# A graph layer with experts on one core: GpSimd writes a small buffer and waits for that write behind each gather and scatter

## The chip, the cores and the metric

The kernel runs on one core of a Trainium2 chip. The time is the device time of one execution in microseconds (us). Engines are named as in the profile: PE is the matmul engine, PEld its weight loads, DVE the vector engine, ACT the scalar engine, POOL is GpSimd, SP the engine that here only issues transfers. Each engine works through its own instructions in order; they wait for each other through semaphores.

## What is computed

There are 6250 nodes with 256 features and 100000 edges, sorted by target node. First a graph layer, then a mixture of experts, both with a residual:

```python
h = layernorm(x)
msg_sum = segment_sum(h[src], dst, N)
deg = segment_sum(ones, dst, N)
agg = msg_sum / maximum(deg, 1)
x = x + concatenate([h, agg], 1) @ W.T + b
xn = layernorm(layernorm(x)) * gamma + beta
logits = xn @ Wr + br                  # 8 experts, the 2 best are taken
w = softmax(top_2(logits))
x = x + sum over the 2 of  w_e * (gelu(xn @ W1[e] + b1[e]) @ W2[e] + b2[e])
```

## The kernel before

**The head** loads x in seven parts, normalises it and writes it to DRAM as `h_rows`, and works out from the edge list which edge tile adds to which node tile.

**The stream** is a loop over a time step t (`for t in range(END)`), which every engine runs through in its own function with its own instructions. Up to STEPS = 830, each t is one step of the segment sum: 128 edges, whose rows of `h_rows` GpSimd has gathered into SBUF with one indirect DMA of 128 rows of 1 KB (L662); PE multiplies them by a one-hot matrix (L764, two passes for float32, so 1660 matmuls) into one of three PSUM banks; DVE adds the bank to the node tile in `acc` (L1125). The first 48 gathers serve two steps each, so there are 782 gathers for 830 steps. The first 63 gathers go to places of their own (`region`); after that they go round a ring of 17 places (`work`). Gather g into the ring's place waits until the step that read the place before is summed (`summed.wait(pool, t - RING)`), and PE waits for the landing of each gather (`got`).

When a node tile is complete, the layer's product, the layernorm, the logits and the choice of experts follow for it a few steps later, on PE, ACT and DVE, between the steps of the sum. Node tiles are closed in 12 batches. For each batch GpSimd scatters its rows to the experts' queues in DRAM, two indirect DMAs for each node tile (L673), one at each t from SCATTER[b] on, so that a scatter comes behind a gather; there are 98. Tiles of 128 queue rows are fetched by SP, multiplied by the expert's weights (L833, L858) and written back as answers, also between the steps of the sum.

**The tail** starts at t = STEPS: the last batches, the remaining experts' tiles, and for each node tile two gathers of its answers (L685, 98), the weighted sum on DVE, and the store of the output.

GpSimd thus has in its stream, in order: 782 gathers with 88 of the scatters among them, then 10 scatters, then 98 gathers of answers. It does nothing else there. The order is written out by hand; no scheduler changes it. `Own(nc, name, engine)` (L31) is a semaphore that an engine raises and waits for itself: `then(i)` lets instruction i raise it and makes the engine wait until it has.

Of the kernel before, what the change touches and what calls it, by code (L numbers as in the profile page):

```python
# [12 lines left out]
P = 128  # L13
# [35 lines left out]
def build(nc, x, src, dst, gnn_w, gnn_b, gamma, beta, wr, br, w1, b1, w2, b2, out):  # L49
    pe, dve, act, pool, sp = nc.tensor, nc.vector, nc.scalar, nc.gpsimd, nc.sync  # L50
# [13 lines left out]
    STEPS = ET + NT - 1  # L64
# [29 lines left out]
    CLEAR = 3  # L94
    FETCH = 6
    PACE = 7


    SIZES = [6, 6, 6, 5, 5, 5, 4, 2, 5, 3, 1, 1]
# [30 lines left out]
    def sb(name, shape, dt=F32):  # L130
        return nc.alloc_sbuf_tensor(name, shape, dt)
# [76 lines left out]
    pslot_i = sb("pslot_i", [1, X], I32)  # L208
    zcol = sb("zcol", [P, 1])
    padrow = sb("padrow", [P, ROW])  # L210
    pcol_i, step_i, qbase_i, e_idx = sb("pcol_i", [P, 1], I32), sb("step_i", [P, GB], I32), sb("qbase_i", [P, X], I32), sb("e_idx", [P, GB], I32)
    bound = sb("bound", [P, 2])

# [109 lines left out]
    d_own, a_own, g_own = Own(nc, "d_own", dve), Own(nc, "a_own", act), Own(nc, "g_own", pool)  # L323
# [20 lines left out]
    def gathered(t):  # L344

        return t - SHARED if t >= BOTH else t // 2 if t % 2 == 0 else None

    def place_of(g):

        return early[:, g, :] if g < SHARED + EXTRA else grow[:, (g - SHARED - EXTRA) % RING, :]  # L350
# [14 lines left out]
    def size(b):  # L365
        return BATCHES[b][1] - BATCHES[b][0]
# [12 lines left out]
    for b in range(NB):  # L379
        t = SCATTER[b] + 2 * size(b) + 7 if SCATTER[b] < STEPS else max(PLACES[b] + 8, STEPS + 5)  # L380
        for j in range(UPTO[b], UPTO[b + 1]):
            if begin_at:
                t = max(t, begin_at[-1] + (PACE if begin_at[-1] + PACE < STEPS else 3))
            begin_at.append(STEPS if STEPS - CLEAR <= t < STEPS else t)
# [12 lines left out]
    def backs(t):  # L397

        return [r for r in range(NT) if BACK[r] == t]

    def back(r, s):

        return grow[:, place_in_ring(STEPS - RING + 2 * (r % PAIRS) + s), 0:D]
# [4 lines left out]
    def answered(engine, j):  # L408

        if j >= 0:  # L410
            engine.wait_ge(s_answer, 16 * (j + 1))
# [226 lines left out]
    def gpsimd_head():  # L638
# [9 lines left out]
        for g in range(GB):  # L648
            pool.indirect_dma_start(tab_i[0:GS, g, :], None, comb, bass.IndirectOffsetOnAxis(e_idx[0:GS, g:g + 1], 0)).then_inc(s_tab, 16)

    def gpsimd_stream():
        pool.wait_ge(s_hst, 16 * NLB)
        srcs_up.wait(pool)
        for t in range(END):
            g = gathered(t) if t < STEPS else None
            if g is not None:
                if g >= RING:
                    pool.wait_ge(got[g % RING], 16 * (g // RING))
                if g >= SHARED + EXTRA + RING:
                    summed.wait(pool, t - RING)  # L660
                cell_of = CELLS + g if g < SHARED else t
                pool.indirect_dma_start(place_of(g)[:, 0:D], None, h_rows,  # L662
                                        bass.IndirectOffsetOnAxis(srcs[:, cell_of:cell_of + 1], 0)).then_inc(got[g % RING], 16)
            for b in range(NB):
                for n in range(2 * size(b)):
                    if t == SCATTER[b] + n:
                        if n == 0:
                            place_up.wait(pool, b)
                            if b == FLUSH + 1:
                                pool.wait_ge(s_pad, 16 * (X + 1))  # L670
                            if b == NB - 1:
                                pool.wait_ge(s_pad, 16 * (2 * X + 1))
                        pool.indirect_dma_start(queue, bass.IndirectOffsetOnAxis(place_i[:, b % 2, n % 2, n // 2:n // 2 + 1], 0),  # L673
                                                pay[:, b % 2, n // 2, :], None).then_inc(s_sent[b], 16)
            for r in backs(t):
                if r == 0:
                    answered(pool, FIRST_TILES - 1)
                if r == CUT:
                    answered(pool, ALL_TILES - 1)
                if r < PAIRS:  # L680
                    summed.wait(pool, STEPS - RING + 2 * r + 1)
                whole_up.wait(pool, r - PAIRS)
                answer_up.wait(pool, r)
                for s in range(2):
                    pool.indirect_dma_start(back(r, s), None, answers[r >= CUT],  # L685
                                            bass.IndirectOffsetOnAxis(answer_i[:, s, r:r + 1], 0)).then_inc(s_pair[r % PAIRS], 16)
# [507 lines left out]
    sync_stream()  # L1194
    scalar_stream()
    gpsimd_stream()
    tensor_stream()
    vector_stream()
# [24 lines left out]
```

## Time and profile before

| | us |
|---|---|
| median of 3 runs | 1425.81 |
| the 3 runs | 1423.88, 1425.81, 1431.27 |
| span of the profiled execution, first to last instruction | 1787.5 |
| PE busy in it | 1241.8 |
| POOL busy in it | 948.0 |
| DVE busy in it | 812.6 |
| ACT busy in it | 463.2 |

The profiled execution is 361.7 us, or 25%, longer than the median of the runs. Its rows give durations and waits of that execution; of the runs only the whole time is known. A row of a timeline gives start, duration, engine, line, operation and tiles; in brackets behind it stands how long the engine was idle before it and what ended that. "issue" there is idle time for which the profile shows no wait, and "remote" one that was ended by something that the profile can't name.

### The profile page before, as it was taken

How to read it: one execution, taken by the hardware profiler on the slowest of the kernel's cores; microseconds unless marked ns; L12 is line 12 of the kernel's file. 1: busy time of each engine (PE TensorE's matmuls, PEld its weight loads, DVE VectorE, ACT ScalarE, POOL GpSimd, SP SyncE). 2: the span in 40 equal slices, each digit the busy share in tenths (PEclk: the TensorE clock that was granted, in tenths of full speed). 3: DMA queues.
4: the chain of work that ended last, by engine and by line, in shares of the span. 5: the costliest groups of instructions: out<-in, count | busy, mean ns of one | idle time of the engine just before them, and what ended most of it. 6: DMA issues, size and time to landing. Idle time of an engine off the chain costs nothing.

```text
span 1787.5 us, 23229 instructions
## 1 busy us (share of the span) xinstructions
PE 1241.8 (69%) x5751; PEld 942.1 (53%) x5751; DVE 812.6 (45%) x2587; ACT 463.2 (26%) x1019; POOL 948.0 (53%) x995
## 2 busy tenths in 40 slices
PE   3223777765874778678787688688788868795881
PEld 2101343442652556556566566566666656684771
DVE  8312663452444445344434444445366565642333
ACT  4200000210220134124124224233322413463440
POOL 3574035666556655655655655665556565115544
PEclk9855998777886889898888889888889889997886
DMA  9732044433333333343333333343344333324553
GB/s 335 247 104 64 1 153 151 133 99 100 110 99 94 107 111 106 115 121 95 113 111 101 110 112 104 109 122 101 115 128 120 105 109 107 101 78 132 160 159 119
DMA packets 128488, 212.63 MB, mean 119 GB/s; under 512 B 25378, under 2 KB 94295, under 8 KB 128119
## 3 DMA queue, kind: packets, MB, share of 16 engines
q0 software_dynamic: 48352, 129.18, 25.2%
q1 hardware_dynamic: 77561, 81.17, 13.7%
q8 instruction: 52, 0.85, 0.2%
q10 hardware_dynamic: 2446, 0.80, 0.2%
q14 instruction: 77, 0.63, 0.1%
HBM read 167.37 MB, written 50.87 MB: 122 GB/s over the span
## 4 chain that ended last, share of the span: by engine, by line
PE 44%; another core or an unknown queue 17%; issue 16%; DVE 11%; ACT 6%; DVEq 2%; DMA 2%; POOL 1%; ACTq 0%; POOLq 0%
PE psum L764 16%; PE psum L833 9%; PE psum L858 8%; DVE acc L1125 5%; PE psum L777 4%; ACT expert_buf L633 2%; PE psum L812 2%; PE psum L778 1%; ACT expert_buf L625 1%; PE psum L845 1%; ACT region L570 1%; DVEq L1118 1%; PE psum L806 1%; PE psum L789 1%
## 5 line engine op out<-in xcount | busy, mean ns | idle before, releaser
L662 POOL DMA_INDIRECT work<-h_rows,srcs x719 | 681.0, 947 | 576.3 <-PE psum L764 324.0
L1125 DVE TENSOR_TENSOR acc<-acc,psum 128x257 f32 x830 | 350.3, 422 | 713.5 <-PE psum L764 329.1
L764 PE MATMUL psum<-work 128*128 128x257 f32 x1438 | 483.6, 450 | 193.7 <-DVE acc L1125 121.9
L764 PEld LDWEIGHTS psum<-work 128*128 128x128 f32 x1438 | 274.7, 219 | 300.3 <-issue 279.1
L833 PE MATMUL psum<-expert_buf 128*128 128x128 f32 x1792 | 235.3, 288 | 40.5 <-ACT expert_buf L625 34.3
L833 PEld LDWEIGHTS psum<-expert_buf 128*128 128x128 f32 x1792 | 230.3, 203 | 50.4 <-ACT expert_buf L625 36.7
L858 PE MATMUL psum<-region,expert_buf 128*128 x896 | 244.7, 422 | 11.6 <-issue 6.5
L633 ACT ACTIVATE expert_buf<-psum,b_col 128x128 f32<-128x128 f32 x448 | 127.8, 370 | 429.7 <-remote 220.0
L858 PEld LDWEIGHTS psum<-region,expert_buf 128*128 128x128 f32 x896 | 186.2, 216 | 49.9 <-issue 21.6
L764 PE MATMUL psum<-region,work 128*128 (+1 forms) x222 | 81.2, 486 | 106.0 <-issue 67.0
L999 DVE TENSOR_TENSOR work<-psum,rel 128x1152 f32<-128x1152 f32 x98 | 126.3, 1289 | 53.6 <-issue 36.7
L685 POOL DMA_INDIRECT work<-answers,answer_i x98 | 93.0, 949 | 108.2 <-DMA answers<-expert_buf 43.5
L625 ACT COPY expert_buf<-region 128x1024 f32 x112 | 117.6, 1050 | 108.7 <-remote 48.2
L673 POOL DMA_INDIRECT queue<-pay,place_i x98 | 97.4, 994 | 85.9 <-DVE place_i L1040 57.7
L580 ACT ACTIVATE acc<-acc,rdeg 128x256 f32<-128x256 f32 x49 | 25.1, 513 | 363.1 <-DVE rdeg L1131 229.5
L777 PE MATMUL psum<-wgt,pair_t 128*128 128x256 f32 x392 | 106.2, 419 | 17.2 <-ACT pair_t L584 11.4
L764 PEld LDWEIGHTS psum<-region,work 128*128 128x128 f32 x222 | 40.8, 220 | 146.0 <-issue 144.0
L1183 DVE TENSOR_TENSOR expert_buf<-psum,b_bc 128x256 f32<-128x256 f32 x112 | 47.2, 422 | 128.2 <-PE psum L858 59.2
L777 PEld LDWEIGHTS psum<-wgt,pair_t 128*128 128x128 f32 x392 | 82.8, 214 | 36.1 <-ACT pair_t L584 15.1
L662 POOL DMA_INDIRECT region<-h_rows,srcs x63 | 59.6, 946 | 35.0 <-issue 18.9
L627 ACT COPY expert_buf<-psum 128x256 f32<-128x256 f32 x112 | 41.6, 371 | 84.8 <-PE psum L845 48.6
L812 PEld LDWEIGHTS psum<-wr_sb,xn_t 128*128 128x128 f32 x196 | 34.6, 242 | 34.8 <-ACT xn_t L610 19.0
(248 smaller groups left out, 896.3 us busy)
## 6 DMA issues: line engine op xcount, KB each, us to landing
expert_buf<-queue SPq DMA_DIRECT2D x112, 128.0 KB
answers<-expert_buf SPq DMA_DIRECT2D x112, 128.0 KB
work<-h_rows,srcs POOLq DMA_INDIRECT x719
region<-in_L_ffn_W_dram SPq DMA_DIRECT2D x16, 512.0 KB
h_rows<-region SPq DMA_DIRECT2D x7, 896.0 KB
own<-h_rows SPq DMA_DIRECT2D x49, 128.0 KB
own<-x_rows SPq DMA_DIRECT2D x49, 128.0 KB
out_dram<-acc SPq DMA_DIRECT2D x49, 128.0 KB
```

What stands on the lines that cost most here:

```text
L625: w1c_up.up(act.copy(w1_now, w1_sb[:, ds(e, 1), :, :].rearrange("p a c h -> p (a c) h")))
L633: i = act.activation(gel[j % 2][:, k * P:(k + 1) * P], hidden(j)[:, k * P:(k + 1) * P], ACT.Gelu, bias=b1_col[:, ds(e + k * X, 1)])
L662: pool.indirect_dma_start(place_of(g)[:, 0:D], None, h_rows, bass.IndirectOffsetOnAxis(srcs[:, cell_of:cell_of + 1], 0)).then_inc(got[g % ...
L673: pool.indirect_dma_start(queue, bass.IndirectOffsetOnAxis(place_i[:, b % 2, n % 2, n // 2:n // 2 + 1], 0), pay[:, b % 2, n // 2, :], None ...
L685: pool.indirect_dma_start(back(r, s), None, answers[r >= CUT], bass.IndirectOffsetOnAxis(answer_i[:, s, r:r + 1], 0)).then_inc(s_pair[r % ...
L764: summed.up(pe.matmul(STEP_BANKS[t % BANKS][:, 0:GW], hot[:, k, :], rows, start=True, stop=True))
L777: pe.matmul(PAIR[:, 0:D], pair_t[:, c * P:(c + 1) * P], wgt[:, c, :], start=(c == 0), stop=False)
L812: i = pe.matmul(ROUTE[:, D + n * X:D + (n + 1) * X], xn_t[:, c * P:(c + 1) * P], wr_sb[:, c, :], start=(c == 0), stop=(c == DC - 1))
L833: i = pe.matmul(hidden(j)[:, units], w1_now[:, c, units], xt[j % 2][:, c * P:(c + 1) * P], start=(c == 0), stop=(c == DC - 1))
L858: i = pe.matmul(result(j), gel[j % 2][:, k * P:(k + 1) * P], w2_sb[:, ds(e, 1), k, :].rearrange("p a o -> p (a o)"), start=(k == 0), stop= ...
L999: hot_up.up(dve.tensor_tensor(hot[:, k0:k0 + n, :], COUNT[:, 0:P].unsqueeze(1).broadcast_to([P, n, P]), rel[:, first:first + n].unsqueeze( ...
L1125: added.up(dve.tensor_tensor(sums, sums, STEP_BANKS[t % BANKS][:, 0:GW], ALU.add))
```

## The change

A scratch buffer of 128 partitions by 24 float32 columns is added. Behind each gather of the stream, and behind each scatter at a step before STEPS, GpSimd writes zeros to it and waits until that write is complete, before it goes on to its next instruction. Nobody reads the buffer. The 10 scatters and 98 gathers of the tail have no such write.

```diff
+    PAUSE = 24
...
+    pause = sb("pause", [P, PAUSE])
...
+    def rest():
+        g_own.then(pool.memset(pause[:, :], 0.0))
+
     def gpsimd_stream():
...
                 pool.indirect_dma_start(place_of(g)[:, 0:D], None, h_rows,
                                         bass.IndirectOffsetOnAxis(srcs[:, cell_of:cell_of + 1], 0)).then_inc(got[g % RING], 16)
+                rest()
...
                         pool.indirect_dma_start(queue, bass.IndirectOffsetOnAxis(place_i[:, b % 2, n % 2, n // 2:n // 2 + 1], 0),
                                                 pay[:, b % 2, n // 2, :], None).then_inc(s_sent[b], 16)
+                        if t < STEPS:
+                            rest()
```

On GpSimd, in the first batch of scatters, the kernel before has gathers (DMA work) and scatters (DMA queue) in turn, directly behind each other; in brackets stands what each waits for:

```order
L662 DMA work<-h_rows,srcs 128x256 [waits summed,got8]
L673 DMA queue<-pay,place_i 54656x256
L662 DMA work<-h_rows,srcs 128x256 [waits summed,got9]
L673 DMA queue<-pay,place_i 54656x256
L662 DMA work<-h_rows,srcs 128x256 [waits summed,got10]
```

In the changed kernel, on GpSimd at the start of a batch of scatters (the lines are 5 or 6 higher):

```order
L667 DMA work<-h_rows,srcs 128x256 [waits summed,got1,g_own]
L654 MEMSET pause 128x24
L679 DMA queue<-pay,place_i 54656x256 [waits place_up,g_own]
L654 MEMSET pause 128x24
L667 DMA work<-h_rows,srcs 128x256 [waits summed,got2,g_own]
L654 MEMSET pause 128x24
L679 DMA queue<-pay,place_i 54656x256 [waits g_own]
```

Between any two of them a write has come in, and the wait for it (`g_own`) is one more wait of the DMA that follows. There are 870 such writes: 782 behind gathers and 88 behind scatters. No instruction of another engine is added or moved.

## Rows read from the trace of the kernel before

**Rows 1.** Busy us of each engine in four stretches; (x) counts instructions.
```profile
core 0: us, PE busy (x) PEld busy (x) DVE busy (x) ACT busy (x) POOL busy (x), PEclk, DMA share, GB/s
59.00:139.00 80.00, 19.75 (x40) 9.71 (x40) 11.03 (x21) 0.00 (x0) 60.09 (x64) 0.62 0.44 134
139.00:243.00 104.00, 63.33 (x193) 32.56 (x193) 52.39 (x113) 0.51 (x1) 15.55 (x18) 0.81 0.15 48
243.00:1515.00 1272.00, 955.38 (x4296) 719.89 (x4297) 598.38 (x1862) 325.33 (x704) 752.61 (x790) 0.85 0.38 112
1515.00:1787.00 272.00, 185.36 (x1129) 166.22 (x1127) 101.96 (x367) 104.10 (x256) 102.74 (x108) 0.85 0.41 124
```
**Rows 2.** Timeline of POOL where the ring is first full, and just behind it.
```profile
157.22 0.94 POOL L662 DMA_INDIRECT work<-h_rows,srcs  x1 [0.30 <-issue]
158.47 0.94 POOL L662 DMA_INDIRECT work<-h_rows,srcs  x1 [0.30 <-issue]
242.99 0.94 POOL L662 DMA_INDIRECT work<-h_rows,srcs  x1 [83.57 <-PE psum L764]
244.23 0.94 POOL L662 DMA_INDIRECT work<-h_rows,srcs  x1 [0.30 <-PE psum L764]
245.48 0.94 POOL L662 DMA_INDIRECT work<-h_rows,srcs  x1 [0.30 <-PE psum L764]
```
**Rows 3.** Timeline of POOL, a gather behind a scatter and a scatter behind that.
```profile
388.52 1.00 POOL L673 DMA_INDIRECT queue<-pay,place_i  x1 [0.30 <-issue]
389.82 0.97 POOL L662 DMA_INDIRECT work<-h_rows,srcs  x1 [0.30 <-PE psum L764]
391.09 1.00 POOL L673 DMA_INDIRECT queue<-pay,place_i  x1 [0.30 <-issue]
```
**Rows 4.** Waits of POOL from 243 to 1515: us in total, times, longest.
```profile
POOL work L662 <- PE psum L764: 324.0, 189, 83.6
POOL work L662 <- issue: 172.6, 477, 4.1
POOL work L662 <- remote: 74.5, 36, 3.1
```
**Rows 5.** Timeline of POOL at the start: its only short writes.
```profile
0.29 0.10 POOL L1211 MEMSET const-float32-1.0<- 128x1 f32 x1
0.32 0.11 POOL L1211 MEMSET const-bfloat16-1.0<- 128x1 bf16 x1
...
0.86 0.86 POOL L639 IOTA work<- 128x888 int32 x1 [0.40 <-POOLq L1211]
1.68 0.12 POOL L640 IOTA pcol_i<- 128x1 int32 x1
1.76 0.12 POOL L641 IOTA step_i<- 128x8 int32 x1
...
1.92 4.59 POOL L643 MEMSET acc<- 128x5397 f32 x1
```
**Rows 6.** Timeline: DVE's write that releases a scatter, and DVE's waits for itself.
```profile
544.47 0.17 DVE L1040 TENSOR_TENSOR place_i<-place,trash 128x12 int32<-128x12 f32 x1
...
544.91 0.99 POOL L673 DMA_INDIRECT queue<-pay,place_i  x1 [0.56 <-DVE place_i L1040]
...
545.86 0.17 DVE L1053 CAST cnt_i<-cnt 128x8 int32<-128x8 f32 x1
546.07 0.17 DVE L1054 TENSOR_SCALAR cnt_i<-cnt_i 128x8 int32<-128x8 int32 x1
```
**Rows 7.** Timeline of a stretch in which PE and DVE stand while POOL issues.
```profile
569.32 0.96 POOL L662 DMA_INDIRECT work<-h_rows,srcs  x1 [0.30 <-issue]
570.43 0.42 DVE L1125 TENSOR_TENSOR acc<-acc,psum 128x257 f32 x1 [4.78 <-remote]
570.59 1.00 POOL L673 DMA_INDIRECT queue<-pay,place_i  x1 [0.30 <-remote]
...
571.00 1.20 PE L764 MATMUL psum<-work 128*128 128x257 f32 x2 [3.54 <-issue]
...
573.16 1.00 POOL L673 DMA_INDIRECT queue<-pay,place_i  x1 [0.30 <-issue]
...
575.21 1.20 PE L764 MATMUL psum<-work 128*128 128x257 f32 x2 [3.02 <-issue]
```
**Rows 8.** Groups of instructions from 243 to 1515: busy, mean ns, idle before and releasers.
```profile
L1125 DVE TENSOR_TENSOR acc<-acc,psum 128x257 f32 x702 | 296.3, 422 | 590.2 <-PE psum L764 310.6 <-remote 183.6 <-issue 54.9
```

## The prediction, made before the changed kernel was run

> **What bounds the kernel now.** I read the busy time of each stretch first [rows 1], then the timeline of POOL [rows 2, 3] and its waits [rows 4]. The change touches GpSimd alone, so the question is how much room GpSimd has.
>
> Of the profiled execution, the stretch from 243 to 1515 us holds the ring's phase: 702 gathers and 88 scatters, 790 POOL instructions. Their busy time is 752.61 us of 1272 [rows 1], which looks like 519 us of room. It is not: behind each gather stand 0.30 us in which nothing else is shown, even where gathers follow one another without a wait, so they start 1.25 us apart (157.22, 158.47; 244.23, 245.48) although each lasts 0.94 [rows 2]. A scatter takes 1.30 to the next start (389.82 less 388.52) [rows 3]. What GpSimd can't go below in this stretch is therefore 702 x 1.25 + 88 x 1.30 = 992 us, and its room is 280 us.
>
> This choice of measure decides the sum. The Trainium skill has the rule in Perfetto Trace Analysis, GPSIMD Engine Instruction: treat a GpSimd span as unreliable and time such instructions from start to start. By that rule the trace agrees with 1.25 and not with 0.95 us; by the durations alone the change would be hidden and the time stay at 1426.
>
> The waits tell the same: from 243 on POOL waited for PE's sum, that is for a free place of the ring, 324.0 us, of which 83.6 are the one wait that ends at 243, and 74.5 for something unnamed [rows 4]. So in the profiled execution the ring is often full, and PE with DVE sets the pace: PE is busy 955.38 of the 1272 us [rows 1].
>
> The runs are another matter. They take 1425.8 us, 361.7 less than the span of 1787.5; what lies around the span is not shown and would make the difference larger. If the shrinking is spread evenly (factor 0.798), the stretch lasts 1272 x 0.798 = 1015 us in a run. A GpSimd DMA is a program's work of fixed length: its spacing is the same 1.25 wherever it is not made to wait, in the quiet stretch ahead of 243 as behind it [rows 2]. I take it to hold in the runs too. Then GpSimd needs 992 of 1015 us: it has **23 us of room, and is all but the bound** of the runs, while PE with 955 has 60.
>
> **The change part by part.** It adds 870 writes with a wait for each. The first 80 (63 places of `region`, 17 of the ring) lie before 243 us, where GpSimd is done at 159.4 and then waits 83.57 us for PE [rows 2]: 80 times any price below is at most 31 us, and that wait hides it. The tail's DMAs have none. 790 remain, one behind each DMA of the ring's phase.
>
> The price of one, x, is not in the trace, since GpSimd never writes between two DMAs and never waits for itself. It has three parts.
> 1. The write. A MEMSET of one column takes 0.10 to 0.11 us, one of 5397 columns 4.59 [rows 5], so 0.85 ns for a column: 24 columns take 0.12 us.
> 2. From the write's end to the next DMA's start. The nearest row is DVE's write of `place_i`, which ends at 544.64 and lets the scatter start at 544.91: 0.27 us [rows 6]. A DVE instruction that waits for its own engine's write starts 0.04 after it (545.86 + 0.17 to 546.07) [rows 6], but it is not a DMA of GpSimd. I take 0.27. It takes the place of the 0.30 that stands there now.
> 3. From the DMA's end to the write's start. Short instructions on GpSimd start behind one another without a gap (1.68 against the end at 1.72) [rows 5]: 0.00. If the 0.30 behind a DMA is work that GpSimd does after it, the write waits for that: 0.30.
>
> So x lies between 0.12 + 0.27 - 0.30 = 0.09 and 0.39 us. Below nothing it can't go by these rows, as the next DMA can't start before the write has ended. I take 0.20, nearer to the low end, because the rows of short instructions show no gap; to this third part the rest of the 0.30 is split about one to two.
>
> Queued behind the waiting GpSimd are its next gather or scatter and nothing else. PE waits for the gather; but it has up to 17 of them in hand, so it is the rate that counts, not the delay of one. The scatter delays the fetch of expert tiles by SP, which is planned several steps later.
>
> The sum: 790 x 0.20 = 158 us, less the room of 23, is **135 us. 1425.8 + 135 = 1561 us.** With x = 0.09 it is 71 - 23 = 48, or 1474; with 0.39 it is 308 - 23 = 285, or 1711. Every DMA then starts 1.45 us after the last, and the ring's phase takes 1150 us. In the profiled execution, with 280 us of room, most of the 158 would be hidden: I expect its span between 1790 and 1870.
>
> **The rivals.**
> *Hidden.* GpSimd's spacing shrinks in the runs as the whole does, to 1.25 x 0.798 = 1.00 us, and x to 0.16. Then it needs 790 x 1.16 = 916 of 1015 us and nothing is lost: 1426 us. For it speaks that nothing of the runs but their whole is known; against it, that the fixed spacing shows no scatter at all, which an engine held up by others would.
>
> *Faster.* There are stretches in which PE and DVE stand for 3 to 5 us at each step while GpSimd issues back to back [rows 7], and DVE's adds lose 183.6 us of the ring's phase to a releaser that the profile can't name [rows 8]. If dense GpSimd DMAs cause these waits, and the runs have them too, a pause between DMAs thins them out. PE's busy time is the floor: at most 1015 - 955 = 60 us come back, 1366 us. It decides where a DMA with its pause stays under 955 / 790 = 1.21 us, which 1.25 alone is over, so GpSimd must also be quicker in the runs than in the trace. Against it speaks too that the runs have hardly room for such waits: PE's 955 already fill 94% of 1015.
>
> *The dear pause.* x is at its upper end, because the write starts only when GpSimd has finished what it does in the 0.30 us. Then 1711 us. For it speaks that the 0.30 appears behind every DMA and behind no short instruction.
>
> That the change does not do what it says is excluded: the writes stand between the DMAs in the order, and the wait is a wait of the DMA behind each.
>
> **How the numbers follow.** The forecast of 1561 (x from 0.05 to 0.3) gets 0.54, the dear pause 0.12, hidden 0.14, faster 0.20. The predicted time is that of the likeliest. The range of 8 in 10 has to take in hidden and most of the dear pause (from 1640 to 1711), and leaves out the greater part of faster: 1400 to 1690. A measurement of this kernel can tell about 0.5% (7 us) from no change. Slower by more is 0.54 + 0.12 = 0.66, the same 0.14, faster 0.20.
>
> **What would show it.** In the profile of the changed kernel: the start-to-start distance of two gathers without a wait, 1.45 (1.34 to 1.64) where it was 1.25; the write's row near 0.12 us; POOL's waits for PE's sum down from 240 us beyond the first to well under 120. If the spacing is 1.45 and the runs are not slower, the spacing of the profiled execution doesn't hold in the runs, and my step from one to the other is wrong. If DVE's unnamed waits fall together with the runs' time, the rival of the thinned waits is right. If the spacing is under 1.30, part 3 is wrong.

## The result and the profile after

The changed kernel takes 1484.03 us (median of 4 runs, 1480.12 to 1489.15), the kernel before 1426.24 (4 runs, 1423.88 to 1431.27). The ratio is 1.0409, with a 95% interval of 1.0379 to 1.0439: 58 us, or 4%, slower. The forecast was slower, by 135 us: the direction and the range hold, the size is more than twice too large.

The first surprise stands in the head of the profile after. Its span is 1481.9 us, as long as its runs, while the profiled execution of the kernel before was 362 us longer than its runs. Busy time and instructions of each engine after:

```profile
span 1481.9 us, 24171 instructions
...
PE 1166.4 (79%) x5751; PEld 891.6 (60%) x5751; DVE 812.8 (55%) x2587; ACT 464.0 (31%) x1019; POOL 1071.5 (72%) x1865
```

The timeline of POOL, which answers to [rows 2], shows the pause as it is (start, duration, and in brackets the idle time before and what ended it):

```profile
240.63 0.95 POOL L667 DMA_INDIRECT work<-h_rows,srcs  x1 [0.27 <-POOL pause L654]
241.58 0.13 POOL L654 MEMSET pause<- 128x24 f32 x1
241.98 0.95 POOL L667 DMA_INDIRECT work<-h_rows,srcs  x1 [0.27 <-PE psum L772]
242.94 0.13 POOL L654 MEMSET pause<- 128x24 f32 x1
243.34 0.95 POOL L667 DMA_INDIRECT work<-h_rows,srcs  x1 [0.27 <-POOL pause L654]
```

A gather lasts 0.95 us as before, the write follows at once (240.63 + 0.95 = 241.58) and lasts 0.13, and 0.27 us after the write's end the next gather starts. Two gathers are 1.355 us apart instead of 1.25: the price of one pause is 0.11 us, not 0.20.

POOL's waits in the whole execution, which answer to [rows 4] (us in total, times, longest):

```profile
POOL work L667 <- POOL pause L654: 164.6, 602, 0.9
...
POOL work L667 <- PE psum L772: 36.3, 112, 1.8
```

For a free place of the ring GpSimd waits for at most 36.3 us, and 112 x 0.27 = 30 of them are the step to the next DMA that stands behind every write. 602 times the release that came last was its own pause.

### The profile page after: what moved, and what is told of

It reads as the page before. It is cut to its first block, busy times and chain, and to the rows that moved or that the text cites. A ratio compares the mean times of both kernels' runs of the same rounds, so it can differ in the third digit from the quotient of the medians.

```text
span 1481.9 us, 24171 instructions
## 1 busy us (share of the span) xinstructions
PE 1166.4 (79%) x5751; PEld 891.6 (60%) x5751; DVE 812.8 (55%) x2587; ACT 464.0 (31%) x1019; POOL 1071.5 (72%) x1865
## 4 chain that ended last, share of the span: by engine, by line
PE 50%; POOL 15%; DVE 11%; issue 9%; DMA 8%; ACT 5%; DVEq 1%; ACTq 0%; POOLq 0%
PE psum L772 14%; PE psum L866 12%; PE psum L841 12%; DMA work<-h_rows,srcs 7%; POOL work L667 5%; PE psum L785 5%; POOL region L667 4%; DVE acc L1133 3%; POOL queue L679 2%; PE psum L820 2%; POOL pause L654 2%; PE psum L786 2%; POOL work L693 2%; ACT expert_buf L635 1%; ACT region L572 1%
## 5 line engine op out<-in xcount | busy, mean ns | idle before, releaser
L772 PE MATMUL psum<-work 128*128 128x257 f32 x1438 | 463.8, 433 | 140.0 <-DVE acc L1133 73.4
L772 PEld LDWEIGHTS psum<-work 128*128 128x128 f32 x1438 | 259.3, 208 | 250.4 <-issue 123.8
L866 PE MATMUL psum<-region,expert_buf 128*128 x896 | 235.1, 409 | 7.4 <-ACT expert_buf L629 5.8
L841 PEld LDWEIGHTS psum<-expert_buf 128*128 128x128 f32 x1792 | 220.6, 195 | 6.7 <-issue 1.7
L841 PE MATMUL psum<-expert_buf 128*128 128x128 f32 x1792 | 223.6, 279 | 0.0
L866 PEld LDWEIGHTS psum<-region,expert_buf 128*128 128x128 f32 x896 | 178.2, 207 | 42.2 <-issue 17.0
L654 POOL MEMSET pause<- 128x24 f32 x870 | 115.1, 132 | 0.7
L785 PE MATMUL psum<-wgt,pair_t 128*128 128x256 f32 x392 | 96.5, 390 | 2.0 <-ACT pair_t L586 2.0
L772 PE MATMUL psum<-region,work 128*128 (+1 forms) x222 | 69.5, 436 | 33.9 <-DVE acc L1133 18.6
L785 PEld LDWEIGHTS psum<-wgt,pair_t 128*128 128x128 f32 x392 | 76.5, 196 | 15.5 <-ACT pair_t L586 4.4
```

Source lines behind the costliest of these rows:

```text
L654: g_own.then(pool.memset(pause[:, :], 0.0))
L772: summed.up(pe.matmul(STEP_BANKS[t % BANKS][:, 0:GW], hot[:, k, :], rows, start=True, stop=True))
L785: pe.matmul(PAIR[:, 0:D], pair_t[:, c * P:(c + 1) * P], wgt[:, c, :], start=(c == 0), stop=False)
L841: i = pe.matmul(hidden(j)[:, units], w1_now[:, c, units], xt[j % 2][:, c * P:(c + 1) * P], start=(c == 0), stop=(c == DC - 1))
L866: i = pe.matmul(result(j), gel[j % 2][:, k * P:(k + 1) * P], w2_sb[:, ds(e, 1), k, :].rearrange("p a o -> p (a o)"), start=(k == 0), stop= ...
```

## Experiments

The prediction's theory, that GpSimd's own pace is the bound, is told apart from its rivals by where the pause stands, by its length, and by GpSimd's work taken away. Each kernel was timed beside the kernel before on the same chip; between groups, ratios to the kernel before are compared.

**Two theories at the start.** Theory A: GpSimd issues without a gap from the first gather to the last and is the bound all along, so that every pause counts. Rival C: it is not the bound, and the time goes in single hand-offs to PE.

**A longer write.**

```diff
-    PAUSE = 24
+    PAUSE = 72
```

> The changed kernel with 72 columns in place of 24 behind each gather and scatter: 48 columns more, 0.04 us by 0.85 ns a column. Theory A (GpSimd issues without a gap from its first gather at 60 us to its last, so every one of the 870 pauses counts in full): distance of two gathers 1.40 us instead of 1.36, 870 x 0.041 = 36 us more than the changed kernel, 1520 us. Rival C (GpSimd is not the bound, the changed kernel loses its time in single hand-offs from GpSimd to PE): a write that is 0.04 us longer leaves the time within 10 us of the changed kernel's 1484.

Measured: 1516.74 us, ratio to before 1.0612 (1.0572 to 1.0652). The write lasts 0.17 us:

```profile
236.46 0.17 POOL L654 MEMSET pause<- 128x72 f32 x1
236.91 0.95 POOL L667 DMA_INDIRECT work<-h_rows,srcs  x1 [0.27 <-PE psum L772]
237.86 0.17 POOL L654 MEMSET pause<- 128x72 f32 x1
238.31 0.95 POOL L667 DMA_INDIRECT work<-h_rows,srcs  x1 [0.27 <-PE psum L772]
```

The distance is 1.40 us. The ratio is 0.020 above the changed kernel's 1.0409, which is 29 us; 870 x 0.041 = 36 were expected. So most of the added 0.04 us a write count once the pauses are there, and rival C, which had at most 10 us, is out.

**The write without the wait.** Three places are written in turn, and each write waits for the one three before it:

```diff
-    pause = sb("pause", [P, PAUSE])
+    pause = sb("pause", [P, 3 * PAUSE])
...
     def rest():
-        g_own.then(pool.memset(pause[:, :], 0.0))
+        n = g_own.count
+        if n >= 3:
+            pool.wait_ge(g_own.sem, n - 2)
+        g_own.up(pool.memset(pause[:, n % 3 * PAUSE:(n % 3 + 1) * PAUSE], 0.0))
```

> The changed kernel with the same 870 writes, but to three places in turn, each write waiting only for the write three before it, which has long ended: the next gather is no longer held by the write's completion. It tells the write from the wait. If the 0.30 us between two DMAs stand in front of each DMA whatever is ahead of it, the distance is 0.95 + 0.13 + 0.30 = 1.38 us and the time 1500 or more; if the write finds room in the 0.30 us, it is 1.25 to 1.28 and the time 1426 to 1440. Theory A: whichever it is, the time follows the distance, 870 us for each us of it.

Measured: 1430.99 us, ratio 1.0016 (0.9997 to 1.0035). POOL's timeline:

```profile
236.37 0.95 POOL L670 DMA_INDIRECT work<-h_rows,srcs  x1 [0.17 <-issue]
237.32 0.14 POOL L657 MEMSET pause<- 128x24 f32 x1
237.63 0.95 POOL L670 DMA_INDIRECT work<-h_rows,srcs  x1 [0.17 <-issue]
```

The write finds its room in the 0.30 us that stand between two gathers anyway: 0.14 of write and 0.17 idle, distance 1.26. So the 870 writes cost next to nothing, and **the wait is the price**: it makes 0.27 us out of the 0.17 behind the write.

**The pause behind the first 80 gathers alone.**

```diff
-                rest()
+                if t < 128:
+                    rest()
...
-                        if t < STEPS:
-                            rest()
```

> The pause only behind the first 80 gathers (steps before 128), none behind scatters. As the prediction had it, these 80 are hidden by the wait of 83.6 us that ends at 243: 1426 us. Theory A: that wait is of the profiled execution alone, in a run GpSimd is not ahead of PE there, and the 80 cost up to 80 x 0.11 = 9 us: 1426 to 1435. In the profile of this kernel, if the pause between the DMAs is what keeps the profiled execution short, the steps up to 128 are as quick as in the changed kernel (step 128 at about 180 us, where the kernel before had it at 264) and the rest is stretched as before.

Measured: 1435.61 us, ratio 1.0050 (1.0030 to 1.0071), so 7 us for 80 x 0.11 = 9. They are not hidden. The profile of this kernel is 1433.8 us long, and not stretched behind step 128 either, though 790 of its DMAs have no pause. The idea that pauses keep a profiled execution short falls with it.

**The pause at the steps before 415.** 403 of the 870:

```diff
-                rest()
+                if t < 415:
+                    rest()
...
-                        if t < STEPS:
+                        if t < 415:
                             rest()
```

> The pause only behind gathers and scatters at steps before 415, 403 of the 870. Theory A: 403 x 0.11 = 44 us more GpSimd time in the first half; room of the first half, about half of 54 us: 44 - 27 = 17, 1443 us. In its profile: the first half of the steps about 620 us long as in the changed kernel, the second stretched as in the kernel before (770 us), span about 1650. If the stretching has to do with the length of the profiled execution or with anything but the distance of the DMAs, both halves are alike.

Measured: 1473.43 us, ratio 1.0320 (1.0282 to 1.0359), which is 45 us: 403 x 0.11 = 44, in full, with no room taken off, where 17 were expected. The profiled span is 1471.3 us, and not the 1650 of an execution that is stretched where the pauses are missing. Since the first half alone gives 45 of the 58 us, the 467 pauses of the second half can add only 13. That is a new theory, E: GpSimd is the bound in the first half of the steps, PE in the second.

**Fewer rows in a gather.** The next two kernels were to make GpSimd's DMAs shorter, first in the kernel before, with 96 rows, then in the changed one, with 112 by the same edit:

```diff
+                rows = 96 if g >= SHARED + EXTRA + RING else P
-                pool.indirect_dma_start(place_of(g)[:, 0:D], None, h_rows,
-                                        bass.IndirectOffsetOnAxis(srcs[:, cell_of:cell_of + 1], 0)).then_inc(got[g % RING], 16)
+                pool.indirect_dma_start(place_of(g)[0:rows, 0:D], None, h_rows,
+                                        bass.IndirectOffsetOnAxis(srcs[0:rows, cell_of:cell_of + 1], 0)).then_inc(got[g % RING], 16)
```

> The kernel before, no pause, but its 702 gathers of the ring's second round on fetch 96 of their 128 rows (the rest of a place keeps what stood there, so the sums are not those of the reference). A gather of 128 rows lasts 0.95 us; if that goes with the rows, one of 96 takes 0.71 and the distance falls from 1.25 to 1.01. Theory A (GpSimd's rate is nearly the bound of the kernel before, with about 54 us of room, and PE's is right behind): the time falls by at most those 54 us or so, until PE binds, to 1370 to 1410. Rival C (GpSimd's rate is not the bound of either kernel): 1426.

> The changed kernel with all its pauses, but its 702 gathers of the ring's second round on fetch 112 of 128 rows (the sums are not the reference's). If a gather's length goes with its rows, it is 0.12 us shorter, which is about what the pause adds (0.11): the distance is 1.24 as in the kernel before. Theory A: the time depends on the distance alone, and is back at 1426 to 1435. If the pause costs in another way (a hand-off to PE that comes later, DVE held by the writes), most of the 58 us stay: 1460 or more.

Measured: 1800.38 us and 1802.75 us, but the kernel before took 1799.27 us beside them (19 runs, 1789.11 to 1808.67): these two ran on another chip than the four above. The ratios are 1.0015 (0.9990 to 1.0039) and 1.0016 (0.9988 to 1.0044). What they were made for they can't tell. They tell two other things. A gather of 96 rows lasts hardly less than one of 128, 0.92 us at a distance of 1.22, so between 96 and 128 rows a gather's length hardly depends on their number:

```profile
253.79 0.92 POOL L663 DMA_INDIRECT work<-h_rows,srcs  x1 [0.31 <-issue]
255.02 0.92 POOL L663 DMA_INDIRECT work<-h_rows,srcs  x1 [0.30 <-issue]
```

And on this chip the kernel before takes 26% longer. The waits there are like those of the first profile [rows 4, 8]; POOL's and DVE's in the kernel with 96 rows, and behind them POOL's in the kernel with 112 rows and all pauses:

```profile
POOL work L663 <- PE psum L765: 330.8, 176, 83.9
...
DVE acc L1126 <- remote: 278.2, 70, 11.4
```
```profile
POOL work L668 <- PE psum L773: 227.9, 117, 59.4
```

The kernel with 112 rows has all 870 pauses, and on this chip no cost of them shows. GpSimd waits there for a free place of the ring for 227.9 us instead of 330.8: the 103 us less are about the pauses' 870 x 0.11 = 96.

**The kernel before, profiled again.** It is unchanged. Two explanations of its first, long profile are told apart: theory D, that chips differ, and rival P, that the profiler stretches this kernel.

> The kernel before, unchanged, profiled again. The first profile of it came from an execution of 1787 us while its runs took 1426; on another chip its runs took 1799. Theory D (chips differ, and the first profile was one of the slower kind): its profiled span is within 1% of its own runs of this call, 1426 or 1799, and where it is 1426, the wait of 83.6 us ahead of the ring's phase is not there and the ring is nearly empty up to step 400 (3 to 9 gathers ahead, as in the kernels with pauses). Rival P (the profiler stretches this kernel, and pauses stop that): the span is about 1790 while the runs beside it take 1426.

Measured: 1432.31 us in its one run, beside seven of 1426.53 to 1432.33, with a profiled span of 1431.0. Rival P is out, and the first profile was of an execution of the slower kind, while the runs shown with it were of the faster kind. That the kind belongs to the chip, as theory D has it, fits but is not shown: no chip was used at two different times, so it could also be a condition that a chip is in for a while. POOL's waits here:

```profile
POOL work L662 <- issue: 160.5, 510, 2.9
POOL work L662 <- PE psum L764: 107.5, 209, 2.7
```

The wait of 83.6 us is gone, and DVE's waits for something unnamed too. The busy times in three stretches (busy us and number for each engine, then clock, DMA share, GB/s), cut at GpSimd's 404th DMA of the stream, which is counted on both sides, and at its last gather:

```profile
61.00:572.00 511.00, 406.70 (x1666) 272.66 (x1667) 288.96 (x792) 98.80 (x204) 383.64 (x404) 0.91 0.48 143
572.00:1207.00 635.00, 546.54 (x2860) 441.34 (x2860) 371.36 (x1204) 226.88 (x501) 444.58 (x467) 0.94 0.45 134
1207.00:1431.00 224.00, 172.91 (x1132) 157.06 (x1130) 104.22 (x368) 104.31 (x257) 105.00 (x109) 0.90 0.51 151
```

The same in the changed kernel, cut at the same DMAs (the POOL counts hold the writes too):

```profile
60.00:615.00 555.00, 427.45 (x1689) 282.81 (x1690) 291.82 (x799) 100.90 (x209) 439.88 (x807) 0.88 0.43 132
615.00:1262.00 647.00, 549.47 (x2841) 439.07 (x2840) 369.04 (x1196) 225.74 (x496) 509.99 (x934) 0.93 0.44 131
1262.00:1482.00 220.00, 171.54 (x1129) 156.02 (x1127) 102.96 (x367) 104.10 (x256) 104.42 (x108) 0.91 0.51 153
```

POOL's DMAs of the kernel before in the first and in the second stretch:

```profile
L662 POOL DMA_INDIRECT work<-h_rows,srcs x305 | 289.0, 947 | 96.0 <-issue 64.9 <-PE psum L764 31.2
L662 POOL DMA_INDIRECT region<-h_rows,srcs x63 | 59.6, 946 | 36.2 <-issue 18.9 <-DMA h_rows<-region 17.3
L673 POOL DMA_INDIRECT queue<-pay,place_i x36 | 35.9, 997 | 12.2 <-issue 9.2 <-DVE place_i L1040 1.8 <-PE psum L764 1.2
```
```profile
L662 POOL DMA_INDIRECT work<-h_rows,srcs x415 | 393.2, 948 | 172.3 <-issue 95.6 <-PE psum L764 76.7
L673 POOL DMA_INDIRECT queue<-pay,place_i x52 | 51.8, 997 | 18.4 <-issue 10.4 <-PE psum L764 4.2 <-DVE place_i L1040 3.9
```

First stretch: 368 gathers x 1.25 + 36 scatters x 1.30 = 507 of 511 us, **room 4**. Second: 415 x 1.25 + 52 x 1.30 = 586 of 635, **room 49**. With the pauses the first grows by 44 us (511 to 555), which is 403 x 0.11 in full; the second by 12 (635 to 647), as 467 x 0.11 = 51 meet 49 us of room, of which about 10 are not used. POOL's gathers of the changed kernel in the second stretch:

```profile
L667 POOL DMA_INDIRECT work<-h_rows,srcs x415 | 396.4, 955 | 121.5 <-POOL pause L654 95.5 <-PE psum L772 19.5 <-issue 6.5
```

With its pause a gather takes 1.355 us to the next start, and a scatter 1.41. That makes 415 x 1.355 + 52 x 1.41 = 636 of the 647 us: in the changed kernel GpSimd sets the pace in the second stretch too, with 11 us left. This is why the longer write cost 29 us, where the first half alone would give 403 x 0.041 = 17: in its trace, cut at the same DMAs, both stretches are longer than in the changed kernel's, by 17 and by 19 us (572 and 665 against 555 and 646). In the first stretch the distances fill 368 x 1.355 + 36 x 1.41 = 549 of 555 us. PE's granted clock falls there from 0.91 to 0.88 and its busy time rises by 21 us, but as GpSimd's distances fill the stretch, that is not what makes it longer.

**The changed kernel again**, unchanged.

> The changed kernel, unchanged, on the chip of this call. Where the kernel before takes 1426 us: 58 us more. Where it takes about 1799 (PE and DVE stand there for long, GpSimd has 280 us of room): by theory D the pause is hidden, a ratio of 1.000 within 0.004.

Measured: 1488.85 us beside 1428.33, ratio 1.0410 (1.0381 to 1.0439).

**The pause at the steps from 415 on**, 467 of the 870; the diff is that of the first half with `t >= 415` behind gathers and `415 <= t < STEPS` behind scatters.

> The pause only behind gathers and scatters at steps from 415 on, 467 of the 870, 467 x 0.11 = 51 us of GpSimd time. Theory E (on a chip where the kernel before takes 1426, GpSimd is the bound in the first half of the steps and PE in the second): most of the 51 are hidden, 13 us stay (the 58 of the whole less the 45 of the first half), 1441 us. Theory A (GpSimd is the bound all along): 1477. On a chip where it takes 1799: nothing.

Measured: 1440.78 us, ratio 1.0086 (1.0063 to 1.0108), 12 us. Theory E had said 1441, theory A 1477. The two halves add up: 45 and 12 make 57 us, and the whole costs 58 to 60.

**Less work for GpSimd.** No pause; 36 gathers of the first half are left out, so that the sums are no longer the right ones:

```diff
+    def left_out(g):
+        t = g + SHARED
+        return 128 <= t < 415 and t % 8 == 0
+
+    def fetched(g):
+        return sum(1 for i in range(g % RING, g + 1, RING) if not left_out(i))
...
-                    pool.wait_ge(got[g % RING], 16 * (g // RING))
+                    pool.wait_ge(got[g % RING], 16 * fetched(g - RING))
...
+                if not left_out(g):
                     pool.indirect_dma_start(place_of(g)[:, 0:D], None, h_rows,
...
-                    pe.wait_ge(got[g % RING], 16 * (g // RING + 1))
+                    pe.wait_ge(got[g % RING], 16 * fetched(g))
```

> The kernel before without 36 of its gathers, every eighth step from 128 to 414 (the step then adds rows of an older gather; the sums are not the reference's). GpSimd has 36 x 1.25 = 45 us less to do in the first half. Theory E: the time falls by up to 45 us, to 1381, less where PE binds first. If GpSimd is not the bound there: 1426. On a chip where the kernel before takes 1799: nothing.

Measured: 1408.47 us, ratio 0.9858 (0.9837 to 0.9880), 20 us faster. GpSimd is the bound in the first half also without any pause, and the next limit comes 20 us behind it: 25 of the 45 us are not given back.

The same with `415 <= t < 830`, 52 gathers:

> The kernel before without 52 of its gathers, every eighth step from 415 on (the sums are not the reference's). GpSimd has 52 x 1.25 = 65 us less to do in the second half. Theory E (PE is the bound there, the ring is full): the time falls by less than 7 us, where 36 gathers fewer in the first half gave 20. Theory A (GpSimd is the bound all along): down by 40 us or more, to under 1390. On a chip where the kernel before takes 1799: nothing.

Measured: 1430.20 us, ratio 1.0011 (0.9989 to 1.0033). With 65 us less of GpSimd's work nothing is gained, so GpSimd is not the bound of the second half of the kernel before; its waits for a free place rise from 107.5 to 164.0 us instead:

```profile
POOL work L670 <- PE psum L772: 164.0, 201, 7.2
```

That PE is what binds there, as theory E says, is argued and not shown. For it speak its busy time, 546.54 of the 635 us against 406.70 of 511 in the first stretch, and the waits for a free place; no run changes PE's work.

**Once more the changed kernel.**

> The changed kernel, unchanged, once more, for the chip of this call. Theory D: where the kernel before takes 1426 the ratio is 1.041, where it takes about 1799 it is 1.000 within 0.004, since GpSimd waits there for a free place of the ring for much longer than 870 x 0.11 = 96 us.

Measured: 1484.34 us beside 1426.84, ratio 1.0398 (1.0370 to 1.0426). This chip, too, is one where the kernel before takes 1427, so the change as it stands was not timed on the slower kind. That it costs nothing there rests on the kernel with 112 rows, whose gathers last 0.94 us instead of 0.95.

## Why the prediction was right in direction and wrong in size

**Right.** The distance from start to start, not the busy time, is what GpSimd can't go below: 1.25 us in the profiles of both kinds. That the runs have far less room than the first profile shows was right, and with it that the kernel gets slower although POOL is idle for nearly half of that profile. Of the price's three parts, the write (0.12 forecast, 0.13 measured) and the step from the write's end to the next DMA (0.27 and 0.27) are as read from [rows 5, 6].

**The price x is the term that was mis-sized.** Part 3, from a DMA's end to the write's start, was set at 0.11, between 0.00 and 0.30, as x = 0.20. It is 0.00, as the rows of short instructions had shown [rows 5]; the 0.30 us are not work that GpSimd does behind a DMA, but a way to the next DMA's start, in which a write can run. So x is 0.11. The forecast counted 790 pauses, and 790 times the difference of 0.09 is 71 of the 77 us by which it was too high. The other 6 are what is left of two further wrong steps with opposite signs: the first 80 pauses, taken as hidden, add 80 x 0.11 = 9, and the room takes 38 us (870 x 0.11 = 96 less the 58 measured) and not 23. That these two nearly cancel is luck.

**"The first 80 are hidden" fell.** The 83.57 us of [rows 2] belong to the slower kind of execution. In the second profile GpSimd runs on without that wait, and the 80 pauses cost 7 of their 9 us.

**"If the shrinking is spread evenly" fell.** I took the longer span for a stretched picture of the run and scaled one stretch by 0.798 to get a room of 23 us. The profile was of an execution in which other waits bound the kernel. In the profile of the right kind the room is 4 + 49 = 53 us, and it is not spread: in the half with 4 us all 44 us of pauses count, in the half with 49 us 39 of 51 are hidden. I had treated the ring's phase as one pool of room.

**What was to be seen in the profile.** The distance was forecast as 1.45 (1.34 to 1.64), and is 1.355. POOL's waits for PE's sum were to fall to well under 120, and are 36.3, but against 107.5 and not 240. The span forecast between 1790 and 1870 was for another kind of execution than the one profiled. The sign for a wrong part 3, a distance under 1.30, could not have shown it: with part 3 at 0.00 the forecast's own parts give 0.94 + 0.12 + 0.27 = 1.33, and its lowest x of 0.09 gives 1.34.

**The rivals.** Hidden is wrong on chips of the faster kind; on the slower the kernel with 112 rows points to it, for its result and not for its reason, since GpSimd's distance does not shrink. Faster is not seen in any time: DVE's unnamed waits are absent from both kernels on the faster kind, and on the slower they stay with the pauses in place. Its first step has something for it on the slower kind, though. In the first profile DVE's adds have these waits from 61 us on, while GpSimd issues, and until 171 us, 12 us after its last gather. From 172 to 243, while GpSimd still stands, there are next to none. The two stretches:

```profile
DVE acc L1125 <- remote: 81.7, 17, 5.9
```
```profile
DVE acc L1125 <- remote: 0.3, 1, 0.3
```

That the DMAs cause them is not shown: no kernel with fewer DMAs ran on the slower kind, and on the faster kind GpSimd issues as densely without such waits. The dear pause is out by the row of the write.

No version that beats both was found. The faster one leaves gathers out; the gain it shows, 20 us, is what fewer GpSimd DMAs in the first half would be worth.

## What to carry to other kernels

Before a profile's waits are scaled to the runs, ask whether it is the same kind of execution: here a span 25% longer than the runs, with the same work, had other waits, and the room read from it was not the room in the runs. Take an engine's room half by half, from the start-to-start distance times the count, because a small cost on every instruction is paid in full where the room is 4 us and mostly hidden where it is 49. And price a wait for one's own write apart from the write: here the write was free and the wait cost 0.10 us, 870 times.

## What the runs showed of the hardware

- The four groups of experiments ran on four chips. On one, the kernel before takes 1799 us (granted clock 0.84 and 0.83 in the two kernels profiled there), on the other three 1427 to 1428 (0.90 to 0.93). The adds on DVE wait there for 278 us in 70 waits of up to 11.4 us whose releaser the profile can't name, and PE is granted less of its clock. What causes these waits was not found, nor whether they belong to the chip or to the time, as each chip was used once. In the kernel with 112 rows and all pauses they are 234 us, and neither the pauses nor fewer rows change the time.
- An indirect DMA of GpSimd for 128 rows of 1 KB lasts 0.95 us, for 96 rows 0.92. Between these sizes its cost is nearly fixed, so there the number of DMAs counts more than their rows.
- The 0.30 us between two such DMAs take up a GpSimd write of 0.14 us in full. With a wait for that write the idle time behind it is 0.27 us, without 0.17.
